# A small U-net of convolutions on one core: level 0's odd map in rows of 33, and another order for VectorE's and ScalarE's last level-0 work

## The reference

```
def basic_block(x, w1, w2, stride=1, ds=None):
    out = relu(conv3(x, w1, stride) * BN_S)
    out = conv3(out, w2, 1) * BN_S
    identity = conv1x1(x, ds, stride) * BN_S if ds is not None else x
    return relu(out + identity)
x = basic_block(x, e0b0c1, e0b0c2)                               # level 0, 64 x 64
x = basic_block(x, e0b1c1, e0b1c2); f0 = x
x = basic_block(x, e1b0c1, e1b0c2, stride=2, ds=e1b0ds)          # level 1, 32 x 32
x = basic_block(x, e1b1c1, e1b1c2); f1 = x
x = basic_block(x, e2b0c1, e2b0c2, stride=2, ds=e2b0ds)          # level 2, 16 x 16
x = basic_block(x, e2b1c1, e2b1c2)
x = (relu(deconv2(x, dec0w) * BN_S) + f1) * BN_S
x = (relu(deconv2(x, dec1w) * BN_S) + f0) * BN_S
```

## Time and profile before

| | |
|---|---|
| median of 3 executions | 91.72 us (91.64 to 91.77) |
| the profiled execution | 91.77 us, its span in the trace 89.9 us |
| granted TensorE clock, mean | 0.983 |
| busy: TensorE / VectorE / ScalarE / GpSimd | 83.3 / 64.0 / 44.8 / 27.5 us |
| stages e0b0c2 and e0b1c2 (48 matmuls each on the odd map) | 11.81 us each |

### The profile page before, as it was taken

One profiled execution on the slowest core, in us unless ns is written; L12 is line 12 of the kernel. 1 busy time (PEld: TensorE's weight loads), 2 busy tenths in 40 slices (PEclk: granted clock), 3 DMA queues, 4 the chain that ended last, 5 costly groups with the idle time before them and its releaser, 6 DMA issues.

```text
span 89.9 us, 1557 instructions
## 1 busy us (share of the span) xinstructions
PE 83.3 (93%) x541; PEld 74.4 (83%) x541; DVE 64.0 (71%) x189; ACT 44.8 (50%) x94; POOL 27.5 (31%) x43
## 2 busy tenths in 40 slices
PE   5988999999999999999999999999999999999900
PEld 3666999998777789999977777999999999887600
DVE  5569999799968799755644559999637798543650
ACT  6006114778445065754423159999920079990410
POOL 7300060999920000555440000300694001500140
PEclk9999999999999999999999999999999999999985
DMA  1879920054674003560000000000000000000075
GB/s 26 245 239 299 293 94 0 0 116 105 178 208 114 19 7 112 161 188 5 0 0 0 0 0 4 0 0 0 0 7 0 4 0 0 7 0 0 0 257 210
DMA packets 4183, 6.51 MB, mean 72 GB/s; under 512 B 464, under 2 KB 2128, under 8 KB 4176
## 3 DMA queue, kind: packets, MB, share of 16 engines
q1 hardware_dynamic: 4032, 6.29, 23.5%
q10 hardware_dynamic: 144, 0.13, 0.4%
HBM read 5.37 MB, written 1.05 MB: 71 GB/s over the span
## 4 chain that ended last, share of the span: by engine, by line
PE 85%; DMA 4%; DVE 3%; SPq 1%; ACT 1%; POOLq 1%; issue 1%
PE psum L838 79%; DMA x_sb<-x_in 4%; PE psum L877 2%; PE psum L975 2%; SPq L418 1%; POOLq L167 1%; PE psum L1030 1%; PE psum L863 1%; DVE stats L612 1%; DVE moments L627 1%; DVE shared L641 1%; ACT result L587 0%; ACT shared L584 0%; PE psum L870 0%; DVE flat L749 0%
## 5 line engine op out<-in xcount | busy, mean ns | idle before, releaser
L470 POOL TENSOR_TENSOR odd<-relu,odd 128x363 fp32r<-128x363 f32 x12 | 13.4, 1131 | 16.0 <-ACT odd L545 16.0
L838 PE MATMUL psum<-shared,w_e0b0c 128*128 128x364 f32 x72 | 12.5, 332 | 0.4 <-DVE shared L641 0.4
L838 PEld LDWEIGHTS psum<-shared,w_e0b0c 128*128 128x128 f32 x72 | 12.0, 188 | 0.7 <-issue 0.7
L838 PE MATMUL psum<-shared,w_e0b1c 128*128 128x364 f32 x72 | 12.2, 329 | 0.0
L838 PEld LDWEIGHTS psum<-shared,w_e0b1c 128*128 128x128 f32 x72 | 12.1, 188 | 0.1
L838 PE MATMUL psum<-odd,w_e0b0c 128*128 128x512 f32 x48 | 12.0, 411 | 0.0
L838 PE MATMUL psum<-odd,w_e0b1c 128*128 128x512 f32 x48 | 12.0, 411 | 0.0
L764 DVE SCALAR_TENSOR_TENSOR relu<-psum,inside 128x363 f32<-128x363 f32 (+2 forms) x18 | 8.7, 488 | 3.8 <-PE psum L838 3.6
L838 PEld LDWEIGHTS psum<-odd,w_e0b1c 128*128 128x128 f32 x48 | 9.1, 190 | 2.6
L838 PEld LDWEIGHTS psum<-odd,w_e0b0c 128*128 128x128 f32 x48 | 9.1, 190 | 2.6
L545 ACT ACTIVATE odd<-relu 128x363 fp32r<-128x363 f32 x12 | 6.2, 519 | 7.0 <-DVE relu L764 7.0
(11 more groups left out here) (126 smaller groups left out, 141.3 us busy)
## 6 DMA issues: line engine op xcount, KB each, us to landing
x_sb<-x_in SPq DMA_DIRECT2D x4, 160.0 KB, 4.0
raw<-e0b0c_in SPq DMA_DIRECT2D x2, 256.0 KB, 4.9
raw<-e0b1c_in SPq DMA_DIRECT2D x2, 256.0 KB, 5.1
raw<-e1b1c_in SPq DMA_DIRECT2D x2, 256.0 KB, 2.7
raw<-e2b1c_in SPq DMA_DIRECT2D x2, 256.0 KB, 2.6
raw<-e1b0c_in SPq DMA_DIRECT2D x1, 448.0 KB, 3.6
raw<-e2b0c_in SPq DMA_DIRECT2D x1, 448.0 KB, 3.8
x_sb<-x_in SPq DMA_DIRECT2D x2, 192.0 KB, 3.9
```

The source lines that it names most:

```text
L470: pool.tensor_tensor(split_of(piece, 1), fp32_of(piece), split_of(piece, 0).bitcast(F32), ALU.subtract).then_inc(lo_ready, 1)
L838: last = pe.matmul(target, w, moving, start=(first and n == 0), stop=(final and n == len(terms) - 1), skip_group_check=skip)
```

## The change

Three edits. The odd map of level 0 has 33 floats a row and not 36. VectorE reads the last level-0 sums (L770 before) ahead of the two remaining side copies of image 0, which it now does between that reading and the low planes; `side_starts` is gone, and image 1's copies are done whole behind the low planes, but for the last, whose start is still ScalarE's. ScalarE does two of image 0's four corners at the old place and two behind its last copies for the sides of image 1.

```diff
-ODD0_PITCH = 36
+ODD0_PITCH = BLOCKS[0] + 1
@@ ScalarE, in the loop over LEVEL0
                 if piece is LEVEL0[-3]:
                     gather_sides(1, 0)
                 if piece is LEVEL0[-2]:
-                    gather_corners(1, 0)
+                    gather_corners(1, 0, range(2))
@@ ScalarE, behind the rests of image 1's sides
             last.then_inc(sides_by_act, 1)
+            gather_corners(1, 0, range(2, 4))
             scale_skip0(0)
             gather_corners(1, 1)
@@ VectorE
-            def side_starts():
-
-                wait_half(dve, LEVEL0[-2].index, 1)
-                first = SIDES_BY_ACT[1, 1]
-                for copy in SIDES[first:-1]:
-                    dve.tensor_copy(*side_copy(1, 1, copy, (0, EARLY_RUN)))
-
             def side_rests():
 
                 first = SIDES_BY_ACT[1, 1]
-                for copy in SIDES[first:]:
-                    last = dve.tensor_copy(*side_copy(1, 1, copy, (EARLY_RUN, RUN[1])))
-                last.then_inc(sides_by_dve, 1)
+                for copy in SIDES[first:-1]:
+                    dve.tensor_copy(*side_copy(1, 1, copy))
+                dve.tensor_copy(*side_copy(1, 1, SIDES[-1], (EARLY_RUN, RUN[1]))).then_inc(sides_by_dve, 1)
@@ VectorE, in the loop over the pieces
                     if piece is LEVEL0[-1]:
-                        side_starts()
+                        side_copies(1, 0, 4, 2)
                     wait_half(dve, piece.index, 0)
@@
-                if piece is LEVEL0[-2]:
-                    side_copies(1, 0, 4, 2)
-                elif piece is LEVEL0[-1]:
+                if piece is LEVEL0[-1]:
                     wait_half(dve, piece.index, 1)
                     side_rests()
```

More of the change, by code:

```diff
@@ L685, in side_copies, with side_rests @@
                     last.then_inc(sides_by_dve, 1)
-            def side_starts():
-                wait_half(dve, LEVEL0[-2].index, 1)
+            def side_rests():
                 first = SIDES_BY_ACT[1, 1]
                 for copy in SIDES[first:-1]:
-                    dve.tensor_copy(*side_copy(1, 1, copy, (0, EARLY_RUN)))
-            def side_rests():
-                first = SIDES_BY_ACT[1, 1]
-                for copy in SIDES[first:]:
-                    last = dve.tensor_copy(*side_copy(1, 1, copy, (EARLY_RUN, RUN[1])))
-                last.then_inc(sides_by_dve, 1)
+                    dve.tensor_copy(*side_copy(1, 1, copy))
+                dve.tensor_copy(*side_copy(1, 1, SIDES[-1], (EARLY_RUN, RUN[1]))).then_inc(sides_by_dve, 1)
             masks([0])
```

## The result

| | before | after |
|---|---|---|
| median | 91.68 us (91.44 to 91.77) | 90.80 us (90.50 to 90.88) |
| profiled execution, its span | 91.77, 89.9 | 90.50, 88.7 |
| ratio after / before | | 0.990, 95% interval 0.987 to 0.993 |

The change is worth about 0.9 us, 1.0%. The forecast was 91.66 us, with a range from 91.05 to 92.05.

The account below looks back on a forecast made before the run. TensorE's matmuls were taken to bound the kernel (busy 93% of the span). The terms 0 + 0.04 - 0.10 + 0 = -0.06 us, on a median of 91.72, gave 91.66 us, range 91.05 to 92.05.

Parts of the forecast that it names:

- Rows of 33, read by TensorE: 96 odd-map matmuls: half the rows stay slow as before, so 0 us, the middle of -0.31 and +0.31.
- all rows fast: Outer bound for the 96 odd-map matmuls: no row slow any more, -0.62 us.
- The first rival: TensorE's odd-map reads: at most a quarter of rows slow, -0.31 to -0.62 us, 91.35 to 91.04 us; chance 0.33.
- VectorE's order: Side copies at e1b0c1: image 1's old wait gone, -0.10 us, new wait at image 0, +0.04 us.
- ScalarE's corners: Two of image 0's corner copies moved later; image 1's end at 65.31 us, cover almost used up: zero.
- ScalarE's and GpSimd's writing: 12 instructions each write 363 elements in one run, not 11 rows; TensorE doesn't wait for them: zero.
- Rivals 2 and 3: Most odd-map rows slow, 91.97 or 92.28 us, chance 0.17; image 0's side casts late, order costing +0.2 us, chance 0.05.

Follow-up runs that it names:

- pitch_only: The kernel before with the odd map's rows of 33 floats alone, without the reordering: 0.9934 (0.991 to 0.996) of before.
- reads33_writes36: Against the kernel before, TensorE alone reads with a step of 33 while ScalarE and GpSimd write rows of 36: 238.4 ns a matmul, 11.44 us for 48.
- order_only: The changed kernel with rows of 36 again, so the reordering alone: 0.9995 (0.998 to 1.002) of before.

## Why the prediction was wrong

**The step that failed** is the first term of the sum, "Rows of 33, read by TensorE". It was put at 0, the middle between -0.31 and +0.31, with -0.62 (all rows fast) as the outer bound. It is -0.80 us, shown by pitch_only and reads33_writes36: a matmul takes 8.3 ns less in the mean, where the prediction called itself wrong from 2 ns on. The step was sound in seeing that this read would decide and that the traced rows begin at only two of four places. It erred twice. First, I took the fast kind's pace, from rows with a gap, for a floor; the trace had none, and one run of 512 gives 233.3 ns, against 241.3 for that kind. Second, I counted each row by its beginning alone. Rows of 37 begin at the same places and take 249.0 ns and not 237.8, so the gap behind a row counts as well. With rows of 33 no piece is left out, and at about every second boundary one row ends in the piece in which the next begins; with rows of 37 none is shared and at every second boundary one is left out. Rows of 35 share none and leave none out, and take 247.2 ns: so 9.4 of the 11.2 ns come before any piece is left out, from the lost sharing or from the wider gap itself, which no run tells apart. The bound was also 13 ns x 48, by modelled durations; by starts the kinds were 9.6 ns apart, so "all rows fast" would have been -0.46.

**The first rival** had the sign and the reason (the wide gap is gone), at 0.33. Its time of 91.04 us for all rows fast lies 0.24 above the median. The remark on 16-byte lines in the Trainium skill (SBUF — State Buffer, Door 1) agrees with the traces in that places within 16 bytes matter: with pitches of 36, 40 and 48, a shift by one float costs 10 to 19 ns. Its condition of two hits on a line isn't borne out: rows of 36 at shift 2 have at least two hits on each line and take 256.7 ns.

**VectorE's order** was right in place and nearly in size: VectorE reads 0.04 us behind the sums (forecast 0.04), image 0's matmuls take 2.88 us (forecast 2.87), image 1's, which no longer wait, 2.80 (forecast 2.82), and e1b0c1 is 0.07 us shorter (forecast 0.06, and 0.06 in order_only). What it missed is that this was the worth at the old pace. At the new pace, the old order loses 0.18 us more (5.93 us in pitch_only, 5.75 before); I priced each part against the trace of before, and two parts of one change priced so don't add up.

**ScalarE's corners**: the copies of image 1 were to end at 65.31 with the load at 65.35; shifted by the 1.24 us by which the last level-0 sums now stand earlier (55.29 for 56.53), that is 64.07 and 64.11, and the trace has 64.09 and 64.14. The cover was indeed used up: from image 1's first shortcut matmul to the next stage's first there are 0.39 us and not 0.37, so 0.02 of the 0.06 us given back behind e1b0c1 are here. The rest I can't place; pitch_only, with the old order, gives back 0.05 us there too.

**ScalarE's and GpSimd's writing** was rightly put at nothing.

**Rivals 2 and 3** did not come. Three in four rows of 33 begin off a multiple of 16 bytes, and in the mean over both shifts their matmuls are the fastest of all that were read in rows, so the beginning alone doesn't make a row slow.

## What to carry to other kernels

When matmuls fill the span, measure how their moving operand is read before anything else: here a pitch of 33 and not 36 floats was worth 0.80 us of TensorE's time, the reordering 0.06 us at the old pace and 0.25 at the new. Padding rows to a multiple of 16 bytes helped only the reads that began there; the closest rows were better in the mean over both shifts, and one run, where the data allows it, would be better still (233.3 ns). And when a change makes the bounding engine faster, price the reordering beside it against the new times: a helper engine that was 0.69 us behind was 0.88 behind afterwards, and that took back a quarter of the gain until the order was changed too.

## What the runs showed of the hardware

- A matmul of 512 fp32r columns comes every 233 ns from one run and every 237 to 257 ns from 16 rows of 32, by pitch and column shift alone, at the same granted clock of 1.00. Where rows lie up to 3 floats apart, each further float of gap costs 4.3 to 5.1 ns (about 1.2 ns for a further 16-byte piece, which is the same thing there).
- Rows 16 floats apart (pitch 48) are read faster in the mean (244.1 ns) than rows 3 floats apart (247.2).
- Two reads whose rows begin at the same places and touch as many 16-byte pieces took 249.9 ns where the gap leaves a piece out (pitch 38, shift 0) and 242.9 where it doesn't (pitch 34, shift 0).
- Four casts on GpSimd slowed VectorE's two casts beside them from 0.92 to 1.42 us, and a low plane from 0.29 to 0.61, so an idle GpSimd was no free helper there. VectorE's reading of sums beside the same casts was not slowed (0.69 us).
- Open: why shifts of 2 and 3 cost 5 ns more than shift 1 at the same pitch, why rows of 38 don't alternate, and what sets the price of a wide gap.
